# Expert stage: 24 shared tiles ahead of the sorted blocks and 8 behind them (before: 16 and 16), and 39 sorted blocks for each half (before: 40)

## The reference: what is computed

```
h = layernorm(x) * (1 + ca) + sa
x = x + ga * windowed_attention(h)        # 16 heads of 64, window of 64
h = layernorm(x) * (1 + cb) + sb
x = x + gb * ffn(h)
```

```
nx      = rmsnorm(X, g2)
rw      = softmax(nx @ Wr.T + expert_bias)            # 8 experts
topw, topi = top_k(rw, 2); topw = softmax(topw)
shared  = swiglu(nx, sW1, sW2, sW3)                   # for every token
special = sum over the 2 experts of topw * swiglu(nx, eW1[e], eW2[e], eW3[e])
return X + shared + special
swiglu(x, w1, w2, w3) = silu(x @ w1.T) * (x @ w3.T) @ w2.T      # 256 -> 256 -> 256
```

## Time and profile before

| what | us |
|---|---|
| median of 3 runs | 2371.08 |
| lowest and highest | 2365.36 and 2372.26 |
| the profiled execution, device time | 2369.41 |
| its span (first to last instruction) | 2367.7 |
| busy in the span: PE | 2058.1 (87%) |
| DVE | 1670.8 (71%) |
| ACT | 1466.2 (62%) |
| POOL | 871.5 (37%) |

### The profile page before, as it was taken

One profiled execution on the slowest core, in us unless ns is written; L12 is line 12 of the kernel. 1 busy time (PEld: TensorE's weight loads), 2 busy tenths in 40 slices (PEclk: granted clock), 3 DMA queues, 4 the chain that ended last, 5 costly groups with the idle time before them and its releaser, 6 DMA issues. The chain is left out here.

```text
span 2367.7 us, 48690 instructions
## 1 busy us (share of the span) xinstructions
PE 2058.1 (87%) x13983; PEld 1786.5 (75%) x13983; DVE 1670.8 (71%) x4189; ACT 1466.2 (62%) x3617; POOL 871.5 (37%) x1569
## 2 busy tenths in 40 slices
PE   2899999988989998369999998699999978689997
PEld 1677777777777777258889897588888867578776
DVE  3577676767767676468888886588888866544658
ACT  2666676766757665237888875378888853345442
POOL 2242333334333332005454552044454434450505
PEclk7899999999999999589999999899999985889999
DMA  3100000000010000700000000000000012143635
GB/s 120 28 15 15 24 21 16 22 19 18 19 32 14 14 15 10 265 28 1 0 0 0 0 0 0 1 1 0 0 0 0 0 47 81 65 163 110 188 103 158
DMA packets 66377, 95.42 MB, mean 40 GB/s; under 512 B 7472, under 2 KB 56496, under 8 KB 66096
## 3 DMA queue, kind: packets, MB, share of 16 engines
q1 hardware_dynamic: 60080, 76.97, 10.2%
q0 software_dynamic: 6144, 16.79, 2.2%
HBM read 51.00 MB, written 38.54 MB: 38 GB/s over the span
## 5 line engine op out<-in xcount | busy, mean ns | idle before, releaser
L398 POOL TENSOR_SCALAR wa_prob<-wa_prob,wa_rinv 128x192 f32<-128x192 f32 x512 | 243.4, 492 | 545.6 <-DVE wa_rinv L567 545.6
L1087 ACT CAST la_pThi<-la_b_t 128x512 fp32r<-128x512 f32 x512 | 293.0, 588 | 141.0 <-PE la_b_t L1387 133.2
L1158 DVE TENSOR_TENSOR la_pTlo<-la_b_t,la_pThi 128x512 fp32r<-128x512 f32 x512 | 341.5, 684 | 42.8 <-ACT la_pThi L1087 40.2
L1031 POOL TENSOR_SCALAR la_prob<-la_prob,la_rinv,la_level 128x1024 f32<-128x1024 f32 x256 | 306.0, 1207 | 78.3 <-DVE la_rinv L1264 78.3
L1255 DVE TENSOR_REDUCE la_nmax<-la_b_s 128x1 f32<-128x1024 f32 x256 | 311.2, 1217 | 24.1 <-PE la_b_s L1376 24.1
L1387 PE MATMUL la_b_t<-la_ident,la_prob 128*128 128x128 f32 x2048 | 303.5, 277 | 11.2 <-DVE la_pTlo L1158 4.7
L1100 ACT ACTIVATE la_prob<-la_b_s,la_nmax 128x1024 f32<-128x1024 f32 x256 | 288.4, 1127 | 7.1 <-DVE la_nmax L1255 5.2
L1387 PEld LDWEIGHTS la_b_t<-la_ident,la_prob 128*128 128x128 f32 x2048 | 235.5, 141 | 62.5 <-DVE la_pTlo L1158 35.5
L1396 PE MATMUL la_b_o<-la_pThi,la_v_st 128*128 128x256 f32 x1024 | 268.8, 296 | 0.0
L1396 PE MATMUL la_b_o<-la_pTlo,la_v_st 128*128 128x256 f32 x1024 | 253.3, 281 | 0.0
L1376 PE MATMUL la_b_s<-la_khi,la_q_now 128*128 128x512 f32 x512 | 221.2, 432 | 12.6 <-ACT la_prob L1100 12.6
(11 more groups left out here) (293 smaller groups left out, 5451.5 us busy)
## 6 DMA issues: line engine op xcount, KB each, us to landing
x_sorted<-la_zeros SPq DMA_DIRECT2D x10, 1024.0 KB
ex_arena<-x_sorted SPq DMA_DIRECT2D x80, 128.0 KB, 2.4
y_sorted<-ex_arena SPq DMA_DIRECT2D x80, 128.0 KB
ex_arena<-in_experts SPq DMA_DIRECT2D x9, 768.0 KB, 4.2
wa_xa<-in_x SPq DMA_DIRECT2D x8, 512.0 KB, 5.1
wa_v_st<-wa_v_st SPq DMA_DIRECT2D x16, 256.0 KB, 3.0
wa_xr<-in_x SPq DMA_DIRECT2D x8, 512.0 KB, 3.9
x_scratch<-wa_xr SPq DMA_DIRECT2D x8, 512.0 KB, 2.7
```

The lines of the kernel that those rows point to most:

```text
L398: x = nc.gpsimd.tensor_scalar(p, p, rinv[:, r, hd:hd + 1], 1.0, ALU.mult, ALU.mult)
L1031: nc.gpsimd.tensor_scalar(p, p, rinv[:, h:h + 1], level[:, h, j:j + 1], ALU.mult, ALU.mult).then_inc(S["pn"], 1)
L1087: nc.scalar.copy(pT[0][:, 4 * j:4 * j + 4, h % 2, :], b_t[j % 2][:].rearrange("p (k n) -> p k n", k=4)).then_inc(S["thi"], 1)
L1158: return nc.vector.tensor_tensor(out, psum, hi.bitcast(F32), ALU.subtract)
```

## The change

The first shared part has 24 tiles (`FIRST = NT + NT // 2`) and the last one 8. A half has 39 sorted blocks. The items are now: 24 shared tiles (0 to 23), 39 blocks of half 0 (24 to 62), 39 of half 1 (63 to 101), 8 shared tiles (102 to 109): 110 items. `COMBINE` is written as before, with the new SPARSE1 = 63 and SHARED1 = 102; the 16 combines of half 1 still begin at SHARED1 + 4, one per loop step. The zero fill writes 13 blocks to a DMA, 3 DMAs for each half. With one line more in the code, lines from 1522 on have a number one higher than before.

```
-NBLK = 40
+NBLK = 39
...
-            EACH = 8
+            EACH = 13
             for rows in A["x_sorted"]:
                 for j in range(0, NBLK, EACH):
...
-        SHARED0, SPARSE0, SPARSE1, SHARED1 = 0, NT, NT + NBLK, NT + 2 * NBLK
+        FIRST = NT + NT // 2
+        SPARSE0, SPARSE1, SHARED1 = FIRST, FIRST + NBLK, FIRST + 2 * NBLK
         ITEMS = 2 * NT + 2 * NBLK

         def tile_of(n):
-            return n if n < SPARSE0 else (n - SHARED1 + NT if n >= SHARED1 else None)
+            return n if n < SPARSE0 else (n - SHARED1 + FIRST if n >= SHARED1 else None)
...
         def shared_before(n):
-            return min(n, NT) + max(n - SHARED1, 0)
+            return min(n, FIRST) + max(n - SHARED1, 0)
```

## The result

The changed kernel takes 2362.41 us (median of 20 runs, 2356.1 to 2369.94); the kernel before has a median of 2369.93 us over 20 runs (2365.36 to 2375.82). The ratio is 0.9969, with a 95% interval of 0.9959 to 0.9978: 7.3 us less (5.2 to 9.7), against 7.8 us worked out; the two medians lie 7.5 us apart. The interval leaves out 0, so the change is real, but it is hardly larger than what the prediction called the limit of telling it from none (7.1 us).

What follows compares the result with a forecast made beforehand. Scatter bounds the front (PE waits 21.0 us), DVE the end, with SP's turns next. 1.95 at the first block plus 5.10 for two blocks, 7.05, plus 0.75 at the end: 7.8 less, 2361.6 or 2363.3; said 2362.3, range 2356.5 to 2368.

Steps and rivals of the forecast that it cites:

- The wait at the first block: PE at the first sorted block's transposes: eight tiles, 20.5 us, fill the 21.0 us wait, leaving 1.7 us.
- The slip of the scatter: POOL's scatter of half 0: tiles beside 14 more intervals make the first block 1.0 us later, bounds 0 to 3.4.
- the upper bound of 3.4: First block's largest lateness, at the scatter pace beside block loads and stores; a 20% rival included this slip, time 2364 to 2367.
- PE is then no longer cold: Behind the first block's transposes: next gate and up after 2.70 us instead of 5.65, saving 2.95 us.
- if PE's clock is still low behind it: Sign that the forecast is wrong: PE's clock still low behind the first block, where full clock was to save 2.95 us.
- One block less in each half: PE's path through the sorted blocks: two items fewer at 2.55 us each, 5.10 us saved.
- SP's turns decide the last part: Output stores and residual loads on SP end last, 3.0 us behind the gathers' chain; eight tiles fewer bring only 0.75 us.
- The rival of denser combines: Last part: denser combines slow each gather interval to 1.44 us, 44.6 us in all; time 2362.0; chance 10%.
- The gathers as the bound: Last part: SP's turns get quicker and the gathers decide; span 2356.9, time 2358.6 us; chance 15%.
- The slower rival: SP's last turns: mean wait for store landings rises from 2.2 to 2.7 us, losing the 7.8 us gain; chance 4%.
- the rival in which the change does nothing: First block late by all the work put ahead, scatters taking 2.9 us each behind the 18th; no gain; chance 1%.

Runs made afterwards that it cites:

- experiment 2: Kernel before with only 24 shared tiles in front and 8 behind (40 blocks, old zero fill): 2365.87 us, ratio 0.9983 to the kernel before.
- experiment 3: Changed kernel with SP's residual load placed one output store later in its last turns: 2359.77 us, ratio 0.9946 to the kernel before.
- experiment 6: Changed kernel with up to 4 scatters in flight instead of 2: 2355.91 us, ratio 0.9949 to the kernel before.
- experiment 5: Kernel before with the zero fill in 4 DMAs of 20 blocks instead of 10 of 8: 2368.26 us, ratio 0.9994 to the kernel before.
- experiment 4: Kernel before with SP's residual load placed one output store later in its last turns: 2369.91 us, ratio 0.9993 to the kernel before.
- experiments 7: Changed kernel with 26 shared tiles in front and 6 behind: 2362.14 us, ratio 0.9973 to the kernel before.
- experiment 9: Changed kernel with 4 scatters in flight and SP's residual load one store later, 24 tiles in front: 2356.70 us, ratio 0.9936 to the kernel before.
- experiment 1: Kernel before with only 39 blocks per half and the zero fill in 6 DMAs, 16 tiles in front and behind: 2365.07 us, ratio 0.9984.
- experiment 8: Changed kernel with 4 scatters in flight, residual load one store later, 23 tiles in front and 9 behind: 2358.68 us, ratio 0.9954 to the kernel before.

## Why the prediction came out

**The time and the bound of the end were right.** 2362.3 was said, 2362.41 measured, and within the part that the change touches 7.8 us were worked out, 7.7 and 8.6 found. That the time was met to 0.1 us is luck: the sum gave 2361.6 or 2363.3, by the base taken, and the runs of one kernel spread over more than 10 us. The terms, one by one:

- *The wait at the first block* shrank as worked out, and the first block did not come earlier. The slip of the scatter was taken as 1.0 us from the pace beside shared tiles (1.411 against 1.335); it was 1.02 and 1.17 in the two profiles. But the cause isn't a steady slowing: POOL waited 0.8 to 2.6 us for single landings instead of the usual 0.3 to 0.45, and in other executions the slip was 2.1 us (experiment 2) and 4.9 (experiment 3), past the upper bound of 3.4. The scatter waits for the landing of the one two before it, so each late landing counts in full (experiment 6). Late landings come without tiles beside them too: in experiment 5, with 16 tiles ahead, the block came after 48.46 us, 1.3 later than before. Only a late one near the end of the half (1.27, 1.00, 1.32 and 2.24 us of waiting ahead of scatter 31 or 32) is seen in all four kernels with 24 tiles and two in flight and in none of the four with 16.
- *"PE is then no longer cold"* was the step that failed: 2.95 us were taken, 0.58 found. It rested on one row, full speed behind an idle time of 1.67 us at the end of the kernel, and that row was read too early. In the same trace the granted clock was 1.00 until about 2357.3, 1.2 us after PE had begun again, and 0.50 from 2357.4 on, while PE was idle once more; the next matmuls of that line took 0.77 us:

```profile
2358.56 0.77 PE L1967 MATMUL ex_b_y<-ex_wxhi,ex_hThi 128*128 128x256 f32 x2 [1.55 <-DVE x_resident L1741]
```

At the first block after, the clock fell in the same way: PE began again at 2075.71 and had 1.00 until 2077.0, then 0.50. And the row is not even steady: in experiment 4, where PE's program is the same, the same two matmuls were already slow:

```profile
2363.32 0.76 PE L1967 MATMUL ex_b_y<-ex_wxhi,ex_hThi 128*128 128x256 f32 x2 [1.67 <-DVE x_resident L1741]
```

So behind 1.54, 1.69 and even 1.11 us of waiting at the first block the clock was low, and by the prediction's own list of signs ("if PE's clock is still low behind it") this step was wrong. Of the 2.4 us that were missing, 0.8 are a second thing that the prediction had not seen: gate and up starts 0.97 us after the transposes instead of 0.14 where the block has only just come. The trace before had it too, behind the transposes at 2078.04:

```profile
2079.01 1.19 PE L1951 MATMUL ex_b_gu<-ex_wxhi,ex_xThi 128*128 128x512 f32 x2 [0.28 <-issue]
```

PE's queue reads the block's expert from the table between the two (L1937; after, a TENSOR_LOAD of 0.50 us from 2075.7 on). In the program that read stands behind the wait for the block, and its time shows when the block arrives less than some 2 us ahead (experiment 6: 0.90 us from transposes to gate and up with full clock). Where the block had been there for longer, the trace has the read ahead of the transposes and 0.14 us (experiments 7 and 9). The rest is the low clock: from gate and up to the next one it was 4.10 us, not 2.54.
- *One block less in each half* was sized at 5.10 us and measured 6.06 in this pair of profiles, 5.8 in the mean of all twelve (experiment 1). The two items are 2.55 each as said; the rest came out of the stretch with combines, 99.96 us before and 99.25 after for 32 items, and out of the first stretch (2.549 against 2.554 for each item). Why these items are a little quicker is open.
- *SP's turns decide the last part*: right, and shown from both sides (experiments 3 and 4). The size was off: the 15 turns were taken as 46.73 us and were 44.78 and 45.6; SP's longest wait for a landing was 2.6 and 2.7 us, not the 3.9 of before. With the landing of the last residual and the end that makes 2.9 us in the first profile and 2.2 in the second, where 0.75 was said.
- *The rival of denser combines* did not come: the gathers took 40.3 and 40.1 us, less than the 41.33 of before, not the 44.6 of that case. *The gathers as the bound* is what experiment 3 makes of it, not this change.
- *The slower rival* needed a mean landing of 2.7 us; it was 33.4/16 = 2.1.
- Two slips of the prediction's working, neither of which bears on the sum: the rival in which the change does nothing is priced at 2.9 us for each scatter behind the 18th, but at that pace the block would come 14 x (2.9 - 1.335) = 22 us later and the kernel would be slower by some 13; about 1.9 to 2.0 us each would do nothing. And the zero fill writes 10240 KB before and 9984 KB after, which is 10.5 and 10.2 MB.

So in the first profile two terms were too small by 1.0 and 2.2 us and one too large by 2.4, and they nearly cancelled. The time was right in part by that luck; the order of the bounds was right by the rows.

## What to carry to other kernels

Work that fills a wait gives back only what the awaited thing gains, not the length of the wait: here 20 us of work were put under the wait, and what came of it was 4.0 us (0.9 to 7.1) by the medians of experiment 2 and nothing in its profile, since the end, too, had three chains within a few us of each other. Before moving work off the end, work out each chain that starts there, DMA turns of an issuing queue included, since a queue that waits for a landing and then issues the next transfer is not on any list of busy engines; let it wait for an older transfer and it falls off the path. And let the awaited thing arrive first, by an item or so: behind a wait of 1.1 us the next item began 5.2 us after the transposes (experiment 8), with the block some 2 us ahead 2.7 us (experiment 9). Last, when a row is to show that a pause did no harm, read on past it: here the rows that answered stood 1.2 and 2.5 us behind the pause.

## What was not expected of the hardware

- Idle times of PE of 1.11, 1.54 and 1.69 us, waiting for a block, were each followed by matmuls at the low clock (0.91 to 1.16 us for a pair that takes 0.71), though PE had been granted 1.00 in all of the 44 us before. The clock did not fall in the wait but 1.1 to 1.3 us after PE had begun again. Near the end of the kernel before it was the same: 1.67 us of idling, then 1.00 for 1.2 us more, then 0.50. With waits of 2.61 and 5.47 us (experiments 2 and 3) the clock was low from the first matmul on. What decides when it falls was not found.
- Single indirect DMAs of the scatter took longer to land than the usual 2.4 us: the longest of half 0 took 3.1 us in the profile before, 3.3 in the one after and 4.7 in experiment 3. With four in flight POOL waited for none, but a late last one (4.5 us, experiment 6) still held back the first block.
- The phase before took from 965.9 to 972.6 us from one execution to the next with the same code, nearly as much as the whole effect of the change. Single profiles had to be compared within the stage.
